# Edge counting in a graph-attention kernel: ScalarE's h copy and x split placed behind the next tile's destination one-hots

## What is computed

```python
h = (x @ W).reshape(n, heads, out_c)           # 1250 x 768
al_s = einsum('nhc,hc->nh', h, a_src)
al_d = einsum('nhc,hc->nh', h, a_dst)
e = leaky_relu(al_s[src] + al_d[dst], 0.2)     # one value per edge and head
m = segment_max(e, dst, num_segments=n)
ex = exp(e - m[dst])
...
out = segment_sum(h[src] * alpha[:, :, None], dst, num_segments=n)
```

## Time and profile before

| What | us |
|---|---|
| median of three runs (1522.79 to 1525.23) | 1523.4 |
| span of the profiled execution | 1518.7 |
| busy over the span: PE / PEld | 1360.8 / 1135.4 |
| busy over the span: DVE / ACT / POOL | 1160.0 / 737.2 / 505.1 |
| L584 PE counting matmuls, busy (576) | 118.6 |
| L601 PE matmuls of h, busy (three groups of 120) | 41.1 + 40.7 + 39.9 |
| L516 DVE source one-hots, busy (192) | 90.9 |
| L545 DVE largest logits, busy (72 and 8) | 100.8 + 11.1 |
| L469 and L476 ACT distances and one-hots, busy | 61.3 + 33.9 |

### The profile page before, as it was taken

The page is one execution under the profiler, slowest core; times in us unless marked ns, Lnnn a source line. Parts: engine busy times, 40 slices in busy tenths (PEclk is TensorE's granted clock), DMA queues, the critical chain, the costliest instruction groups (busy, mean ns, idle before and its releaser), DMA issues. The chain is left out here.

```text
span 1518.7 us, 31335 instructions
## 1 busy us (share of the span) xinstructions
PE 1360.8 (90%) x7728; PEld 1135.4 (75%) x7739; DVE 1160.0 (76%) x1823; ACT 737.2 (49%) x1171; POOL 505.1 (33%) x557
## 2 busy tenths in 40 slices
PE   6888888888778889889977999999999999999995
PEld 4555656733223348889967999999999999999995
DVE  6499999899999988858878477555565655888882
ACT  3556465255555553422224455444454544666662
POOL 1000000003333410032324555555465555555563
PEclk9999999799999999999977999999999999999998
DMA  6300001041222214233566987867778876799963
GB/s 233 138 18 9 18 28 61 18 179 61 73 95 63 78 44 141 63 105 106 127 166 216 269 223 204 186 166 170 171 193 205 203 191 159 210 271 273 254 135 49
DMA packets 102255, 211.68 MB, mean 139 GB/s; under 512 B 19318, under 2 KB 58486, under 8 KB 102082
## 3 DMA queue, kind: packets, MB, share of 16 engines
q1 hardware_dynamic: 79186, 142.06, 28.7%
q0 software_dynamic: 22240, 66.69, 22.0%
q10 hardware_dynamic: 784, 2.36, 0.4%
HBM read 164.14 MB, written 54.93 MB: 144 GB/s over the span
## 5 line engine op out<-in xcount | busy, mean ns | idle before, releaser
L992 PE MATMUL ps_o<-prob,h_head 128*97 128x512 f32 (+1 forms) x480 | 187.7, 528 | 51.5 <-DVE prob L934 51.5
L2070 POOL DMA_INDIRECT out_nodes<-y,to_index x92 | 160.1, 1740 | 133.9 <-issue 73.5
L2387 PE MATMUL ps_h<-e_hi,e_xt_hi 128*128 (+1 forms) x546 | 192.6, 353 | 6.3 <-ACT e_xt_hi L2189 3.6
L992 PEld LDWEIGHTS ps_o<-prob,h_head 128*97 128x97 f32 x480 | 73.2, 164 | 165.4 <-issue 89.7
L2372 PE MATMUL ps_y<-e_hi,e_ht_hi 128*128 (+1 forms) x546 | 191.6, 351 | 3.6 <-DVE e_ht_lo L2305 2.2
L2387 PE MATMUL ps_h<-e_lo,e_xt_hi 128*128 (+1 forms) x546 | 184.7, 338 | 0.0
L2372 PE MATMUL ps_y<-e_hi,e_ht_lo 128*128 (+1 forms) x546 | 183.6, 336 | 0.0
L2372 PE MATMUL ps_y<-e_lo,e_ht_hi 128*128 (+1 forms) x546 | 183.5, 336 | 0.0
L2254 DVE TENSOR_TENSOR e_lo<-raw,e_hi (+1 forms) x189 | 175.6, 950 | 7.3 <-ACT e_hi L2197 6.7
L2207 ACT ACTIVATE y<-ps_y,gate 128x768 f32 (+1 forms) x91 | 82.2, 903 | 192.4 <-PE ps_y L2372 124.2
L826 ACT ACTIVATE score<-score,al_col 128x1250 f32<-128x1250 f32 x80 | 106.0, 1335 | 98.4 <-DVE score L877 98.4
(11 more groups left out here) (357 smaller groups left out, 3053.0 us busy)
## 6 DMA issues: line engine op xcount, KB each, us to landing
raw<-in_ew SPq DMA_DIRECT2D x192, 384.0 KB, 5.7
w_room<-rel_dram SPq DMA_DIRECT2D x14, 640.0 KB, 4.6
b_all<-in_eb SPq DMA_DIRECT2D x32, 192.0 KB
al_src<-al_dram SPq DMA_DIRECT2D x1, 5000.0 KB, 14.6
xs<-in_x SPq DMA_DIRECT2D x5, 768.0 KB, 12.5
x_in_t<-in_x SPq DMA_DIRECT2D x10, 384.0 KB, 3.7
out_nodes<-x SPq DMA_DIRECT2D x10, 384.0 KB, 4.2
table<-xf SPq DMA_DIRECT2D x10, 384.0 KB, 2.7
```

The lines of the kernel that those rows point to most:

```text
L992: turn = nc.tensor.matmul(ps_o[u][0:C1 + 1, c, 0:WID[c]], h_head[:, u, t, :], prob[:, t % 2, 512 * c:512 * c + WID[c]], start=(t == 0), st ...
L2070: nc.gpsimd.indirect_dma_start(out, bass.IndirectOffsetOnAxis(to_index[:, w:w + 1], 0), y[:, w, :], None, bounds_check=NP - 1, oob_is_err= ...
L2387: nc.tensor.matmul(ps_h[:, 0:HID], xt_hi[:, c, :], b[:, bass.ds(e % 2, 1), c * HID:(c + 1) * HID] .rearrange("p o m -> p (o m)"), start=(c ...
```

## The change

It is on ScalarE alone. The copy of h and the split of x become a function `keep_h(t)`. It is called in the iteration of the next tile, behind that tile's destination one-hots and ahead of `keep_turned`; the last tile's call stands behind the loop. Inside the loop body the six instructions get another order: the first pair's one-hot now stands behind the third distance, where it was behind the fourth. The waits are the same, taken singly.

```diff
+                def keep_h(t):
+
                     act.wait_ge(h_summed, t + 1)
                     for half in range(2):
                         last = nc.scalar.activation(
...
                     last.then_inc(h_kept, 1)
                     if t + 2 < NT:
                         split_x(t + 2)
...
-                        for pair in range(2):
-                            act.wait_ge(dst_made, m + (pair + 1))
-                            for q in range(2):
-                                last = nc.scalar.activation(away[:, pair, q, :], s.column[:, t * P:(t + 1) * P],
-                                                            ACT.Abs, bias=s.dst_neg[:, bass.ds(2 * e + 2 * pair + q, 1)])
-                            last.then_inc(away_made, 1)
-                        for pair in range(2):
-                            act.wait_ge(away_made, m + (pair + 1))
-                            if pair:
-                                act.wait_ge(onehot_used, m + 2)
-                            nc.scalar.activation(one_dst[:, slots[pair]].rearrange("p o q n -> p (o q n)"),
-                                                 away[:, pair].rearrange("p q n -> p (q n)"),
-                                                 ACT.Relu, bias=1.0, scale=-1.0).then_inc(dst_made, 1)
...
+                        act.wait_ge(onehot_used, m + 1)
+                        act.wait_ge(dst_made, m + 1)
+                        distance(0, 0)
+                        distance(0, 1).then_inc(away_made, 1)
+                        act.wait_ge(dst_made, m + 2)
+                        distance(1, 0)
+                        act.wait_ge(away_made, m + 1)
+                        one_hot(0)
+                        distance(1, 1).then_inc(away_made, 1)
+                        act.wait_ge(away_made, m + 2)
+                        act.wait_ge(onehot_used, m + 2)
+                        one_hot(1)
                         act.reg_add(made, made, 2)
                     if t == 0:
                         split_x(0)
                         split_x(1)
                     if t:
+                        keep_h(t - 1)
                         keep_turned(t - 1)
                         act.wait_ge(mask_made, t)
                         act.wait_ge(turned, t)
                     act.wait_ge(counted, t + 1)
                     nc.scalar.activation(counts[:, 0:1024], ps_c[:, 0:2, :].rearrange("p a n -> p (a n)"), ACT.Copy)
                     nc.scalar.activation(counts[:, 1024:NP], ps_c[:, 2, 0:256], ACT.Copy).then_inc(counts_kept, 1)
+                keep_h(NT - 1)
                 keep_turned(NT - 1)
```

## The result

The changed kernel takes 1514.53 us (median of four runs, 1510.61 to 1517.82) against 1523.67 us for the kernel before beside it: a ratio of 0.9931 with a 95% interval of 0.9916 to 0.9947, so 10.5 us less (8 to 13); the two medians are 9.1 apart. The profiled execution spans 1512.0 us, 6.7 less than the one of before. 1512.8 had been forecast, out of a stage shortened by 10.7 us (the forecast took off 10.6). The time alone does not tell this forecast from the first rival's 1516.2; the stage's own rows do.

A forecast was written before the change was run, and what follows sets the result against it. VectorE was taken as the longer engine, with TensorE's late start, behind ScalarE's one-hots, reaching it through the ring. Gains of 0.2 + 2.2 + 8.3 = 10.7 us, rounded to 10.6, took 1523.4 to 1512.8 us; range 1510.4 to 1517.5.

The forecast's parts named there:

- first rival: Counting still starts 1.87 us behind the source one-hots' start; gain 7.2 us, 1516.2 us; chance 0.13.
- Tile 0: First tile: only the new body order counts, VectorE's source pair becomes the later one; 0.2 us gained.
- Tile 1: Second tile: only ScalarE is late, so TensorE's whole idle time before counting goes; 2.2 us gained.
- Tiles 2 to 8: Steady tiles: VectorE's first pair becomes the late one, period 22.05 us; 8.3 us gained.
- P - D: P starts a tile's counting on TensorE, D its source one-hots on VectorE; gap forecast at 1.33 us.
- The copies that move back: ScalarE's later h copy and x split: h out of PSUM 8.5 us after counting starts, 4.6 us of cover.
- The second pair inside a body: ScalarE's second one-hot directly behind its distance: 0.1 to 0.3 us more per body, nothing on the path.
- The end: Stage end, tile 9: VectorE stays last, its end moves by 10.7 us, and all is handed on.
- The clock: TensorE's half-clock stretches: one in tile 3's counting cost nothing; 2 us allowed both ways in the range.
- Late start remains: Something between ready pair and matmul keeps TensorE's counting late; gain 7.2 us, 1516.2 us; chance 0.13.
- only the lead: Only tiles 0 and 1 gain, the steady period stays; gain 2.4 us, 1521.0 us; chance 0.06.
- The h copy comes too late: ScalarE's ring wait delays the h copy past counting, TensorE stands before h; 3.2 us lost, 1526.6 us; chance 0.05.

The follow-up runs named there:

- E11: Changed kernel with 28 spare copies on ScalarE ahead of the h copy in each tile; 1563.6 us.
- E4: Changed kernel with one of VectorE's eight largest-logit reductions cut to a tenth of its columns; 1506.1 us.
- E5: Kernel before the change with one of VectorE's eight largest-logit reductions cut to a tenth of its columns; 1522.5 us.
- E1: Kernel before with only the new order inside the loop body, h copy and x split left in place; ratio to before 0.9982.
- E3: Kernel before with only the x split moved behind the next tile's one-hots, h copy left ahead of them; 1524.7 us.
- E8: Changed kernel with 14 spare copies on ScalarE ahead of the h copy in each tile; 1513.0 us.
- E2: Changed kernel with the old order inside the loop body, so only the h copy and x split move; ratio to before 0.9909.
- E10: Changed kernel with the mask of tiles 0 to 8 made on GpSimd instead of VectorE; ratio to before 1.012.

## Why the prediction held

*Tile 0: 0.2 forecast.* P moved from 54.03 to 53.39, of which 0.3 was there before the stage: 0.34. As worked out, the source pair is now the later one.

*Tile 1: 2.2 forecast, 3.1 measured.* Two things were mis-sized. The idle time of 2.17 in the earlier trace rows is counted from the modelled end of the zero matmuls, but a ready matmul need not wait for that. Zero matmuls to counting are 2.67 before (72.14 to 74.81) and 0.33 after (71.50 to 71.83), 2.34. And TensorE, with its sequencer already inside the loop, did the first 24 matmuls in 4.68 us without the stop of 0.3 between bodies that it makes elsewhere; the tile's counting took 12.7 us instead of 13.5. D of tile 2 is 92.18, 3.7 earlier (3.4 without the 0.3), where 2.4 was forecast. In E11, where TensorE's long wait lets the sequencer run ahead in every tile, counting is 0.4 to 0.7 us shorter in all of them.

*Tiles 2 to 8: 8.3 forecast, 8.1 measured.* From D of tile 2 to D of tile 9 are 154.83 us, 162.94 before; behind that, 0.2 more is gained. P - D is 1.32 (1.33 forecast), the period 22.0 to 22.1 (22.05). One tile takes 22.5; it is the one that was 23.6 before, and that extra stayed, as allowed for. E4 and E5 show that the pace is VectorE's after and wasn't before, and E1 that ScalarE's chain set it before; E3 adds that the chain's middle term is ScalarE's loop entry. The prediction's sentence that VectorE is the longer engine was right in length, but the one that TensorE's late start reaches it through the ring is only half of it: before, nothing of VectorE's was on the path (E5), and its ring waits were slack used up.

*The copies that move back.* h out of PSUM at P + 8.5 forecast, P + 8.3 measured (123.80 against 115.53); cover 4.6 forecast, and at least that in E8. What I had not seen is that the split's 0.84 us cost nothing where it was (E3).

*The second pair inside a body.* Each body has 0.17 us more wait before its second one-hot, and 1.95 us became 2.24: nothing on the path.

*The end.* TensorE's chain ends at 277.1 and VectorE's at 280.3; VectorE stayed last, by more than forecast, since the 96 small matmuls took 10.83 us instead of 12.54. The half clock does this: six of them take 0.51 us at full clock and 0.96 at half, and in before half clock begins 3.3 us into them (0.53 granted from 282 to 292 us), in after 5.3 us (0.54 from 271 to 277).

```profile
266.24 10.83 PE L628 MATMUL ps_h<-att_col,w_cols 128*96 128x2 f32 x96
```

*The clock.* The half-clock stretch in tile 3 is gone: from 60 to 270 us the granted clock is 1.00 after. That it had cost nothing, as the prediction read from tiles 2 and 3, holds for that tile, which made it up: its first 48 matmuls went through in 10.59 us without a stop between bodies, where tile 2 stops 0.28 us at each. It is no rule for counting. In tile 0 of E2 half clock lasted beyond 58 us (0.80 granted from 58 to 62 us, 1.00 in after), and counting took 1.0 us longer.

*The rivals.* "Late start remains" fell with P - D = 1.32, "only the lead" with the period. "The h copy comes too late" wasn't reached. The sum was 1.1 us too small in the stage, nearly all of it tile 1's, and 1512.8 against 1514.5 lies within what the part behind the stage varies by; that the time came so near is in part luck, since the two differences have opposite signs. That this part would move by 2 us either way was too narrow: it moved by 6 among executions. The range's lower end is also not quite its terms' own: 0.3 + 2.2 + 8.9 us and the 2 us of the clock give 1510.0, not 1510.4.

## What to carry to other kernels

When an engine's list holds a wait for work that is late and, behind it, preparation that needs nothing of that work, put the preparation first; then ask how late the moved copy may come, and test that distance with spare work. Price a move by the chain it shortens and not by the moved instruction: the x split lay over its engine's own loop entry and was free, while the wait in front of the h copy was not. When the wait is gone, look up who is late by the smallest amount next and give some of its work to the engine that has just been freed: here that gave over half as much again (6.8 us of the stage beside 11.8).

## What the hardware showed that I had not expected

- An engine's entry into a loop with run-time bounds takes its sequencer over a microsecond behind a wait: 1.40 us from the start of the h copy to the first distance with nothing in between (E3). In after it takes as long behind `counted`, 1.42 us from counts copy to first distance (106.86 to 108.28), but the two counts copies fill all but 0.1 of it.
- A copy of 128 columns that waits for its neighbour through a constant took 0.33 us from start to start; the second one-hot of a body, behind a wait against a register, starts 0.17 us after its distance has ended, 0.56 after its start. Which of the differences between the two cases makes this is not shown.
- TensorE's stand of 4.4 us before h (E11) brought half clock upon the matmuls behind it in every tile and raised the loss a tile from 3.6 to 5.4 us. Behind the waits of 1.9 us of before there was one such stretch in tiles 1 to 9 (0.76 granted from 120 to 124 us), and behind those of 0.8 in after none.
- GpSimd's 4.66 us elementwise instruction stopped VectorE's one-hots for 4.2 us (E10).
